# Two cross-attention and expert layers on one core: in the first attention the values are weighed head by head, across group borders

## The chip, the cores and the metric

The kernel runs on one core of a Trainium2 chip. The metric is the device time of one execution in microseconds (us), the median of several. The profile shows one execution; its engines are PE (TensorE, matrix products), DVE (VectorE), ACT (ScalarE), POOL (GpSimd) and SP (which only issues transfers).

## The reference, cut to what matters

Two layers, each a cross-attention and a mixture of experts, on 2048 tokens (2 batches of 1024) of width 256. The change touches the first attention alone:

```python
def _L0_xattn_ref(query, key, value, mask, wq, bq, wk, bk, wv, bv, wo, bo):
    Q = proj(query, wq, bq, sq)          # 16 heads of width 16
    K = proj(key, wk, bk, sk)            # 154 keys
    V = proj(value, wv, bv, sk)
    scores = jnp.einsum('bhqd,bhkd->bhqk', Q, K) / np.sqrt(D_K)
    scores = jnp.where(mask[:, None, :, :] == 0, NEG, scores)
    attn = jax.nn.softmax(scores, axis=-1)
    ctx = jnp.einsum('bhqk,bhkd->bhqd', attn, V)
    return ctx.transpose(0, 2, 1, 3).reshape(b, sq, D_MODEL) @ wo + bo
...
x = x + _L0_xattn_ref(_layernorm(x), ctx_1024, ctx_1024, mask, ...)
x = x + _L0_ffn_ref(_layernorm(x), ...)   # 8 experts, the best 2 of each token
```

## The kernel before, in words

Every engine has its own instruction list, written by hand, and waits on counted semaphores (`pe.wait_ge(S("a0_mx"), n)` waits until n maxima are taken). An engine runs its list strictly in the order written. The order of the calls in the loops over `g` and `u` is therefore the schedule.

The tokens are worked in four groups (`g` 0 to 3, NG) of four tiles (`t`) of 128 tokens. A group of the first attention has these steps.

- Queries. `turn` transposes the normalised tokens, `project_q` makes the queries in two banks of PSUM (there are 8 banks of 512 numbers; which two, `q_bank(g)` says), ACT's `q_parts` and DVE's `q_low` split them in a high and a low half-precision part, and SP's `stack_queries` carries them through memory into `q_stack`. This is done two groups ahead, near the end of group g-2.
- Maxima. `score_max(g, n)` makes scores with the tokens on the partitions, and DVE's `maximum(g, n)` takes the largest of each token and head. This is done one group ahead. Then DVE's `negate`, PE's `turn_max` and ACT's `maxima_turned` bring the maxima into the rows of `edge`.
- Scores. `score(g, u)` makes scores with the keys on the partitions, a unit of 512 tokens at a time: 16 units for the 16 heads' first 128 keys, and 4 units that each hold the last 26 keys of four heads. The units use banks 4 and 5 in turn. ACT takes the exponential of a unit (L1160) into a ring of four, then copies it to half precision (`p_hi`, L1163); DVE forms the rest (`p_lo`, L1690). The exponential of unit u waits for the rest of unit u-4.
- Weighing. `weigh_values(g, t)` multiplies the weights of one tile, all heads, by the values, 40 matrix products for a tile, and ACT's `low_outputs`, DVE's `head_outputs` (L1541, L1542, L1545) add the parts and divide by the sum.
- Output. `turn_out` and `project_out` for each half group (two tiles), and DVE's `update` adds it to `x` (counted by a0_x). The rows then get their statistics (`moments`, `scale_and_shift`), `turn_rows` and `route_rows` make the logits of the experts, DVE's `choose` and `place` (with `route_positions` on PE between them) pick experts and places, and POOL's `split_rows` and `scatter` write the rows to the experts' lists. These run one group late, beside the next group's scores. POOL's `low_parts` makes low parts of the first expert's weights once the scores of group 2 are done.

Before, all 20 units of a group are scored first and kept (`p_hi` and `p_lo` hold 20 units each), and the four `weigh_values` follow at the group's end. The loop of PE:

```python
for u in range(20):
    score(g, u)
    if more and 1 <= u < 13:
        score_max(g + 1, u - 1)
...
weigh_values(g, 0)
weigh_values(g, 1)
if more:
    turn_max(g + 1)
```

The maxima are taken in 12 steps of up to six heads, each over two banks; the steps use banks 0 and 1, and 2 and 3, in turn. The experts' layer begins when the rows of the last group are scattered; that waits for the last `update` of the first attention.

## Time and profile before

| what | value |
|---|---|
| median of 3 executions | 921.59 us (919.04 to 923.31) |
| the profiled execution's own time | 923.3 us |
| its span, first to last instruction | 921.6 us |
| mean granted clock of PE | 0.879 |
| busy over the span | PE 77%, DVE 61%, ACT 44%, POOL 32% |
| first attention, from the first rest of a unit to the last update of x | 58.5 to 264.3 us of the span |

A row of a timeline is: start in us, length in us, engine, line, operation, output and inputs by name with shapes, how many; in brackets the engine's idle time before it and what ended it. The length runs over the pipeline's fill and drain, so that rows on one engine may overlap; the distance of two starts is what one instruction costs in a row of them.

### The profile page before, as it was taken

How to read it: one execution, taken by the hardware profiler on the slowest of the kernel's cores; microseconds unless marked ns; L12 is line 12 of the kernel's file. 1: busy time of each engine (PE TensorE's matmuls, PEld its weight loads, DVE VectorE, ACT ScalarE, POOL GpSimd, SP SyncE). 2: the span in 40 equal slices, each digit the busy share in tenths (PEclk: the TensorE clock that was granted, in tenths of full speed). 3: DMA queues.
4: the chain of work that ended last, by engine and by line, in shares of the span. 5: the costliest groups of instructions: out<-in, count | busy, mean ns of one | idle time of the engine just before them, and what ended most of it. 6: DMA issues, size and time to landing. Idle time of an engine off the chain costs nothing.

```text
span 921.6 us, 19114 instructions
## 1 busy us (share of the span) xinstructions
PE 708.8 (77%) x6266; PEld 552.5 (60%) x6278; DVE 560.0 (61%) x1396; ACT 403.0 (44%) x720; POOL 293.2 (32%) x285
## 2 busy tenths in 40 slices
PE   5676786987744999998997989995762098889882
PEld 4223454554534898887885878895441076767771
DVE  7778586887653645564645646457687445566441
ACT  1135465766430635463545535443443045445331
POOL 6415201416258213122212122121045414333342
PEclk8788898978666999999998999997755589999996
DMA  4661303302336523534535523415023455464332
GB/s 134 122 138 39 58 1 62 135 23 77 118 112 234 149 44 63 145 76 127 126 77 152 143 63 94 107 26 174 23 79 111 160 166 125 103 149 118 54 58 39
DMA packets 68419, 92.25 MB, mean 100 GB/s; under 512 B 14442, under 2 KB 54435, under 8 KB 68348
## 3 DMA queue, kind: packets, MB, share of 16 engines
q1 hardware_dynamic: 41788, 63.37, 23.2%
q0 software_dynamic: 14592, 16.24, 10.4%
q10 hardware_dynamic: 11968, 11.72, 4.9%
q8 instruction: 42, 0.69, 0.3%
q14 instruction: 29, 0.24, 0.1%
HBM read 64.21 MB, written 29.87 MB: 102 GB/s over the span
## 4 chain that ended last, share of the span: by engine, by line
PE 42%; DVE 26%; issue 13%; ACT 8%; DMA 4%; ACTq 2%; POOL 2%; another core or an unknown queue 1%; DVEq 1%; POOLq 0%; SPq 0%
PE ps L659 40%; DVE probs L1690 2%; DVE stats L1357 2%; DVE mx L1553 2%; DVE keys L1768 2%; DVE probs L1773 2%; ACT probs L1163 1%; DMA out_x<-keys,row_to 1%; DMA probs<-rows 1%; POOL rows L612 1%; DVE keys L1747 1%; ACT expo L1160 1%; ACT probs L1241 1%; ACT probs L1245 1%
## 5 line engine op out<-in xcount | busy, mean ns | idle before, releaser
L1768 DVE TENSOR_TENSOR keys<-probs,ps 128x512 f32<-128x512 f32 x122 | 82.7, 686 | 191.6 <-PE ps L659 121.8
L659 PE MATMUL ps<-keys,slot 128*128 128x256 f16 (+1 forms) x1440 | 149.5, 266 | 15.5 <-issue 8.9
L659 PE MATMUL ps<-keys,probs 128*128 128x256 f16 (+1 forms) x1488 | 139.9, 255 | 19.2 <-issue 15.6
L659 PEld LDWEIGHTS ps<-keys,slot 128*128 128x128 f16 x1440 | 128.5, 100 | 35.6 <-issue 17.5
L659 PEld LDWEIGHTS ps<-keys,probs 128*128 128x128 f16 x1488 | 123.6, 98 | 34.6 <-issue 19.9
L575 POOL DMA_INDIRECT attended<-keys,row_to x42 | 68.9, 1641 | 167.6 <-ACT keys L1253 145.4
L1241 ACT ACTIVATE probs<-ps 128x512 f32<-128x512 f32 x122 | 71.4, 598 | 79.9 <-PE ps L659 75.3
L1253 ACT ACTIVATE keys<-ps,carried 128x256 f32<-128x256 f32 x80 | 33.5, 470 | 150.4 <-issue 84.4
L1245 ACT CAST probs<-keys 128x512 f16<-128x512 f32 x122 | 74.8, 614 | 26.8 <-DVE keys L1768 24.2
L1773 DVE TENSOR_TENSOR probs<-keys,probs 128x512 f16<-128x512 f32 x122 | 83.5, 688 | 3.8 <-ACT probs L1245 2.0
L1690 DVE TENSOR_TENSOR probs<-expo,probs 128x512 f16<-128x512 f32 x80 | 61.8, 784 | 33.1 <-ACT probs L1163 29.7
L659 PE MATMUL ps<-slot,probs 128*128 128x256 f16 x636 | 75.6, 273 | 3.4 <-ACT probs L1245 2.3
L659 PE MATMUL ps<-probs 128*128 128x256 f16 x612 | 72.7, 273 | 2.8 <-ACT probs L1245 2.1
L575 POOL DMA_INDIRECT out_x<-keys,row_to x38 | 58.9, 1550 | 48.4 <-ACT keys L1253 41.6
L1160 ACT ACTIVATE expo<-ps 128x512 f32<-128x512 f32 x80 | 48.1, 601 | 52.7 <-PE ps L659 44.1
L659 PEld LDWEIGHTS ps<-slot,probs 128*128 128x128 f16 x636 | 59.7, 98 | 15.2 <-ACT probs L1245 4.6
L659 PEld LDWEIGHTS ps<-probs 128*128 128x128 f16 x612 | 57.5, 98 | 13.9 <-ACT probs L1245 4.6
L571 POOL COPY row_to<-carried 128x2 int32 x40 | 11.9, 298 | 155.3 <-DMA attended<-keys,row_to 55.9
L907 PE MATMUL ps<-identh,probs 128*128 128x128 f16 x336 | 26.5, 224 | 34.2 <-DMA probs<-rows 34.2
L1367 DVE TENSOR_TENSOR probs<-inbox,probs 128x1024 f16<-128x1024 f32 x36 | 43.3, 1222 | 13.4 <-ACT probs L1103 13.4
L659 PE MATMUL ps<-penalties,identb 128*128 128x462 bf16 x96 | 34.5, 360 | 19.2 <-DVE mx L1553 7.7
L1163 ACT CAST probs<-expo 128x512 f16<-128x512 f32 x80 | 49.0, 618 | 0.0
(277 smaller groups left out, 1147.6 us busy)
## 6 DMA issues: line engine op xcount, KB each, us to landing
inbox<-in_W SPq DMA_DIRECT2D x24, 512.0 KB
probs<-rows ACTq DMA_DIRECT2D x44, 260.0 KB
inbox<-in_wg SPq DMA_DIRECT2D x16, 512.0 KB
inbox<-in_wu SPq DMA_DIRECT2D x16, 512.0 KB, 3.8
inbox<-in_wd SPq DMA_DIRECT2D x16, 512.0 KB, 4.2
rows<-zeros SPq DMA_DIRECT2D x16, 260.0 KB
x<-in_x SPq DMA_DIRECT2D x4, 512.0 KB, 6.3
q_out<-queries SPq DMA_DIRECT2D x8, 256.0 KB, 2.1
```

What stands on the lines that cost most here:

```text
L575: pool.indirect_dma_start(out=l.sums, out_offset=bass.IndirectOffsetOnAxis(ap=row_to[:, hf:hf + 1], axis=0), in_=yb[:, hf, :], in_offset=N ...
L659: return pe.matmul(o, l, r, start=start, stop=stop, **kw)
L907: last = pe.transpose(psh[:, 6, part * BLK + hf * P:part * BLK + (hf + 1) * P], x_raw[:, hf, part * P:(part + 1) * P], identh[:, :])
L1160: act.activation(e_ring[:, u % 4, :], ps[:, 4 + u % 2, :], ACT.Exp, scale=float(DK) ** -0.5).then_inc(S("a0_exp"), 1)
L1163: act.copy(p_hi[:, u - 1, :], e_ring[:, (u - 1) % 4, :]).then_inc(S("a0_phi"), 1)
L1241: act.activation(s_act[:, j % 2, :], ps[:, 2 * (j % 2), :], l.act).then_inc(S(r + "_s"), 1)
L1245: act.copy(h_hi[:, 2 * j - 2:2 * j, :].rearrange("p c t -> p (c t)"), h32[:, (j - 1) % 2, :]).then_inc(S(r + "_hh"), 1)
L1253: ins = act.activation(yb[:, hf, :], ps[:, 4 + hf, 0:D], ACT.Identity, scale=carried[:, bass.ds(g, 1), hf, 0:1].rearrange("p b d -> p (b d)"))
L1367: dve.tensor_tensor(w[:, 1, at:at + CH], stage[:, n % STAGES, :], w[:, 0, at:at + CH], ALU.subtract).then_inc(S(f"w_ready{l.n}"), 1)
L1690: dve.tensor_tensor(p_lo[:, u, :], e_ring[:, u % 4, :], p_hi[:, u, :], ALU.subtract).then_inc(S("a0_plo"), 1)
L1768: dve.tensor_tensor(h32[:, j % 2, :], s_act[:, j % 2, :], ps[:, 2 * (j % 2) + 1, :], ALU.mult).then_inc(S(r + "_h32"), 1)
L1773: dve.tensor_tensor(h_lo[:, 2 * j - 2:2 * j, :].rearrange("p c t -> p (c t)"), h32[:, (j - 1) % 2, :], h_hi[:, 2 * j - 2:2 * j, :].rearran ...
```

## The change

The four `weigh_values` at a group's end are gone. The 20 units are reordered as four head groups of five: four heads, then the unit with their last 26 keys. `weigh_unit(k, i)` weighs one unit for all four tiles (8 matrix products) and stands in PE's loop five to seven units behind its score, so that the last head group of a token group is weighed beside the first units of the next. After each head group `low_outputs(k)` and `head_outputs(k)` run for all four tiles, 16 times in all as before and with the same number of elements. The outputs of the weighing keep banks 2 and 3, so that the maxima have only banks 0 and 1: 24 steps of at most three heads, each in one bank, in units 1 to 10 (`max_steps`) instead of 12 steps in units 1 to 12. The rings `p_hi` and `p_lo` hold ten units. `choose` and `place` of group g move from the end of group g+1 into units 2 and 7 of group g+2, `route_rows` to unit 1 of it. In DVE's loop the maxima of unit n+2 now stand ahead of the rest of unit n. Other steps move by some units, and some buffers to other places.

```diff
+QH = 4
+UNITS = 5 * QH
+HELD = 10
+STEPS = 24
...
         def q_bank(g):
-            return 6 if g == 1 else 2
+            return 6 if g else 2
...
+        def weighed_heads():
+            tiles = ps[:, 2:4, :].rearrange("p b (t c) -> p (b t) c", c=D)
+            return tiles[:, :, 0:QH * VW].rearrange("p t (h v) -> p t h v", v=VW)
+
+        def max_steps(u):
+            return range(STEPS * (u - 1) // 10, STEPS * u // 10) if 1 <= u <= 10 else range(0)
+
+        def weighed_at(n):
+            k, step = divmod(n - 7, 5)
+            units = (range(0, 2), range(2, 4), range(4, 5), range(0), range(0))[step] if k >= 0 else range(0)
+            return [(k, i) for i in units if k < QH * NG]
...
+            def weigh_unit(k, i):
+                g, q, n = k // QH, k % QH, 5 * k + i
+                b, slot = g // 2, n % HELD
+                pe.wait_ge(S("a0_plo"), n + 1)
+                if i == 0:
+                    if k:
+                        pe.wait_ge(S("a0_oev"), k)
...
+                for t in range(GT):
+                    o, tk = o4[:, t], slice(t * P, (t + 1) * P)
+                    if i < QH:
+                        mm(o[:, i, :], p_hi[:, slot, tk], v_ext[:, b, QH * q + i, :], i == 0 and t % 2 == 0, False, ...)
+                        last = mm(o[:, i, 0:DK + 1], p_lo[:, slot, tk], v_ext[:, b, QH * q + i, 0:DK + 1], False, False, ...)
...
             for g in range(NG):
-                for u in range(20):
+                for u in range(UNITS):
                     score(g, u)
-                    if more and 1 <= u < 13:
-                        score_max(g + 1, u - 1)
+                    for k, i in weighed_at(UNITS * g + u):
+                        weigh_unit(k, i)
+                    if more:
+                        for n in max_steps(u):
+                            score_max(g + 1, n)
+                    if g >= 2 and u == 1:
+                        route_rows(g - 2, range(GT), g - 1)
...
+                    if ahead and u == 18:
...
+                        project_q("a0", g + 2, w_sb["wq"], q_bank(g + 2))
...
-                weigh_values(g, 0)
-                weigh_values(g, 1)
...
@@ ACT
+                    if u % 5 == 4 and UNITS * g + u >= 9:
+                        low_outputs((UNITS * g + u - 9) // 5)
@@ DVE
+                    if n == 0:
+                        maxima(1)
+                    maxima(n + 2)
+                    dve.wait_ge(S("a0_phi"), n + 1)
+                    dve.tensor_tensor(p_lo[:, n % HELD, :], e_ring[:, n % 4, :], p_hi[:, n % HELD, :], ALU.subtract)...
+                    if u % 5 == 4 and n >= 9:
+                        head_outputs((n - 9) // 5)
+                    if g >= 2 and u == 2:
+                        choose(L[0], g - 2)
+                    if g >= 2 and u == 7:
+                        place(L[0], g - 2)
```

On DVE, at the border of groups 0 and 1, before: the last rests of group 0 (L1690), the queries' low parts (L1531), and the first of the four head outputs; the first rest of group 1 and the first maximum come behind the fourth.

```order
L1690 TENSOR_TENSOR probs<-expo,probs 128x512 x2
L1531 SCALAR_TENSOR_TENSOR queries<-ps,b_bq,queries 128x512 x2
L1690 TENSOR_TENSOR probs<-expo,probs 128x512
L1704 TENSOR_TENSOR gate<-gate,ps 128x32
L1541 TENSOR_TENSOR heads<-ps,heads 128x256
L1542 RECIPROCAL rden<-ps 128x16
L1545 TENSOR_TENSOR heads<-heads,rden 128x256
```

The same place on DVE now, from the last two rests but one of group 0 (L1725 is the rest, L1579 a maximum of one bank, L1559 the queries' low part).

```order
L1725 TENSOR_TENSOR probs<-expo,probs 128x512 x2
L1579 TENSOR_REDUCE mx<-ps 128x3 x2
L1725 TENSOR_TENSOR probs<-expo,probs 128x512
L1569 TENSOR_TENSOR heads<-ps,heads 128x256
L1570 RECIPROCAL rden<-ps 128x16
L1573 TENSOR_TENSOR probs<-heads,rden 128x4x64
L1559 SCALAR_TENSOR_TENSOR queries<-ps,b_bq,queries 128x512 x2
L1579 TENSOR_REDUCE mx<-ps 128x3 x2
L1725 TENSOR_TENSOR probs<-expo,probs 128x512
```

Two maxima of the group after next moved ahead of the group's last rest, one head output stands there in place of four, and the queries' low part comes behind it.

On PE, in unit 11 of group 0, before: the score (slot,keys; turned_masks; edge), and right behind it a maximum step over two banks (penalties; keys,queries), as in each of the units 1 to 12.

```order
L659 MATMUL ps<-slot,keys 128x512
L659 MATMUL ps<-turned_masks,identb 128x512
L659 MATMUL ps<-edge,msel 128x512
L659 MATMUL ps<-penalties,identb 128x462
L659 MATMUL ps<-keys,queries 128x308
L659 MATMUL ps<-keys,queries 128x154
L659 MATMUL ps<-penalties,identb 128x462
L659 MATMUL ps<-keys,queries 128x462
```

On PE, from unit 8 to unit 9 of group 0 now: a maximum step in one bank, then the score of the last keys of four heads, and behind it the weighing of a unit (probs with v_rem; the pair of products comes four times, once for a tile, of which the first stands here).

```order
L678 MATMUL ps<-penalties,identb 128x462
L678 MATMUL ps<-keys,queries 128x462
L678 MATMUL ps<-gate,mean 128x8 x4
L678 MATMUL ps<-slot,k_rest 128x512 x2
L678 MATMUL ps<-edge,mselr 128x512
L678 MATMUL ps<-v_rem,probs 128x132
L678 MATMUL ps<-v_rem,probs 128x4x17
```

The weighing stands between a unit's score and its maximum steps.

On ACT, at the border of groups 1 and 2, before: from the last but one exponential of group 1 to the first two of group 2.

```order
L1160 ACTIVATE expo<-ps 128x512
L1163 CAST probs<-expo 128x512
L1093 ACTIVATE queries<-ps,b_bq 128x512 x2
L1122 COPY xT<-ps 128x1024
L1160 ACTIVATE expo<-ps 128x512
L1163 CAST probs<-expo 128x512 x2
L1110 ACTIVATE xln<-x,nb_r,ry_r 128x256 x4
L1138 COPY heads<-ps 128x256
L1097 ACTIVATE ev<-dv 128x4
L1138 COPY heads<-ps 128x256
L1142 COPY edge<-ps 32x512
L1138 COPY heads<-ps 128x256 x2
```

The same place on ACT now.

```order
L1187 ACTIVATE expo<-ps 128x512
L1193 CAST probs<-expo 128x512
L1164 COPY heads<-ps 128x256
L1151 COPY xT<-ps 128x1024
L1193 CAST probs<-expo 128x512
L1122 ACTIVATE queries<-ps,b_bq 128x512 x2
L1139 ACTIVATE xln<-x,nb_r,ry_r 128x256 x4
L1187 ACTIVATE expo<-ps 128x512 x2
L1193 CAST probs<-expo 128x512
```

Three of four head copies left the border, and the queries' high part (L1122) moved behind the last exponential and the copy of the turned rows (L1151).

## Rows read from the trace of the kernel before

**Rows 1.** Windows: the four groups and the tail (columns in the first line)

```profile
core 0: us, PE busy (x) PEld busy (x) DVE busy (x) ACT busy (x) POOL busy (x), PEclk, DMA share, GB/s
58.50:113.00 54.50, 38.71 (x302) 20.21 (x303) 40.03 (x83) 27.55 (x52) 21.10 (x17) 0.86 0.41 79
113.00:164.30 51.30, 41.48 (x347) 25.41 (x350) 38.23 (x104) 31.31 (x61) 4.56 (x8) 0.93 0.20 48
164.30:208.00 43.70, 38.43 (x332) 24.43 (x333) 36.34 (x101) 30.21 (x57) 14.28 (x18) 0.88 0.17 60
208.00:238.60 30.60, 22.96 (x100) 12.14 (x99) 24.68 (x42) 21.89 (x43) 14.67 (x13) 0.87 0.41 126
238.60:264.30 25.70, 16.57 (x206) 14.20 (x206) 9.85 (x49) 4.51 (x11) 12.16 (x17) 0.62 0.20 66
```

**Rows 2.** Groups of instructions of DVE, 164.3 to 208.0 us, by form

```profile
L1690 DVE TENSOR_TENSOR probs<-expo,probs 128x512 f16<-128x512 f32 x20 | 13.4, 688 | 3.6 <-ACT probs L1163 3.5
L1553 DVE TENSOR_REDUCE mx<-ps 128x6 f32<-128x924 f32 x8 | 8.9, 1114 | 0.0
L1555 DVE TENSOR_REDUCE mx<-ps 128x3 f32<-128x462 f32 x4 | 2.5, 633 | 0.0
L1545 DVE TENSOR_TENSOR heads<-heads,rden 128x256 f32<-128x256 f32 x4 | 1.7, 425 | 0.1
L1541 DVE TENSOR_TENSOR heads<-ps,heads 128x256 f32<-128x256 f32 x4 | 1.7, 424 | 2.9 <-ACT heads L1138 2.8
L1556 DVE TENSOR_REDUCE mx<-ps 128x1 f32<-128x154 f32 x4 | 1.2, 310 | 0.0
L1542 DVE RECIPROCAL rden<-ps 128x16 f32<-128x16 f32 x4 | 1.0, 248 | 0.0
```

**Rows 3.** Timeline of ACT at the border of groups 1 and 2

```profile
145.85 0.60 ACT L1160 ACTIVATE expo<-ps 128x512 f32<-128x512 f32 x1 [3.50 <-PE ps L659]
...
147.84 1.28 ACT L1093 ACTIVATE queries<-ps,b_bq 128x512 f16<-128x512 f32 x2
149.00 1.03 ACT L1122 COPY xT<-ps 128x1024 f32<-128x1024 f32 x1
149.89 0.64 ACT L1160 ACTIVATE expo<-ps 128x512 f32<-128x512 f32 x1
...
162.48 1.24 ACT L1160 ACTIVATE expo<-ps 128x512 f32<-128x512 f32 x2 [0.28 <-PE ps L659]
```

**Rows 4.** Timeline of PE: a projection of queries, and one of logits

```profile
141.49 3.67 PE L659 MATMUL ps<-xT,w_wq 128*128 128x512 f32 x8 [1.55 <-ACT xT L1086]
...
236.34 2.47 PE L659 MATMUL ps<-gate,xT 128*128 128x8 f32 x16 [1.60 <-ACT xT L1122]
```

**Rows 5.** Timeline: a maximum and the step that waits for it

```profile
47.65 1.11 DVE L1553 TENSOR_REDUCE mx<-ps 128x6 f32<-128x924 f32 x1
...
48.82 0.37 PE L659 MATMUL ps<-penalties,identb 128*128 128x462 bf16 x1 [0.33 <-DVE mx L1553]
```

**Rows 6.** Timeline of group 3, while POOL makes low parts

```profile
217.54 8.73 DVE L1690 TENSOR_TENSOR probs<-expo,probs 128x512 f16<-128x512 f32 x3 [0.61 <-issue]
...
218.22 6.29 POOL L561 TENSOR_TENSOR slot<-inbox,slot 128x1024 f16<-128x1024 f32 x3
...
225.16 0.60 ACT L1160 ACTIVATE expo<-ps 128x512 f32<-128x512 f32 x1 [4.58 <-DVE probs L1690]
```

**Rows 7.** Timeline of DVE in the tail: first and last of choose, of place

```profile
242.03 0.18 DVE L1576 COPY lg<-ps 128x32 f32<-128x32 f32 x1
...
244.47 0.17 DVE L1608 TENSOR_TENSOR cumb<-cumb,gsum 128x8 bf16<-128x8 bf16 x1
...
249.73 0.22 DVE L1616 TENSOR_TENSOR ohp<-oh,ps 128x64 f32<-128x64 f32 x1
...
250.85 0.17 DVE L1636 TENSOR_TENSOR xp<-dn,xp 128x4 f32<-128x4 f32 x1
```

**Rows 8.** Timeline of the tail: the last low copy, the last update

```profile
256.26 0.37 ACT L1138 COPY heads<-ps 128x256 f32<-128x256 f32 x1 [7.53 <-remote]
...
263.56 0.69 DVE L1571 TENSOR_TENSOR x<-x,ps 128x512 f32<-128x512 f32 x1 [4.91 <-PE ps L659]
```

More of the change, by code:

```diff
@@ L1172, in _ @@
                         normalise("a0", g + 2, 3)
-                    if g + 2 < NG and u == 15:
+                    if g and u == 12:
+                        out_turned(g - 1, 1)
+                    if ahead and u == 13:
                         x_evac("a0", g + 2, xT)
-                    if g + 2 < NG and u == 18:
+                    if more and u == 16:
+                        maxima_turned(g + 1)
+                    if g and u == 19:
+                        rows_turned(g - 1, range(GT), 0, g)
+                    if ahead and u == 20:
                         q_parts(g + 2)
-                    if g and u == 18:
-                        rows_turned(g - 1, range(GT), 6, g)
                     if g == NG - 2 and u in (4, 7, 9):
@@ L1681, in _ @@
             q_low(0)
-            for n in range(12):
+            for n in range(STEPS):
                 maximum(0, n)
@@ L1706, in _ @@
                                           ALU.subtract).then_inc(S("kv_done"), 1)
[L1707 removed]
+                    if g and u == 12:
                         update(g - 1, 0)
[L1709 removed]
+                    if g and u == 15:
                         update(g - 1, 1)
[L1711 removed]
+                    if g and u == 16:
                         dve.wait_ge(S("a0_x"), 2 * g)
                         moments("r0", (g - 1) * GT, GT)
[L1714 removed]
+                    if g and u == 17:
                         scale_and_shift("r0", (g - 1) * GT, GT)
[L1716 removed]
+                    if ahead and u == 19:
                         q_low(g + 2)
[L1718 to L1727 removed]
+            choose(L[0], NG - 2)
+            head_outputs(QH * NG - 1)
+            place(L[0], NG - 2)
+            update(NG - 1, 0)
             dve.wait_ge(S("a0_x"), 2 * NG - 1)
```

319 lines of the change are left out of this document (145 added, 174 removed).

## The prediction, made before the changed kernel ran

> **What bounds the kernel now.** I read the windows first, cut at the first rest of each group (p_lo, L1690). From there to the last update of x the first attention takes 205.8 us, in pieces of 54.5, 51.3, 43.7, 30.6 and, for the tail behind the last rest, 25.7 [rows 1]. Over these DVE is busy 40.0, 38.2, 36.3, 24.7 and 9.9 us, together 149.1, PE 158 and ACT 115. No engine is full: DVE stands for 56.7 us, 14.5, 13.1 and 7.4 in the first three groups and 21.8 in the last with its tail. The reader is to see that the engines wait for each other, and where.
>
> The first place is the group border. The last exponential of group 1 starts at 149.89, the first of group 2 at 162.48, 12.6 us later, with the weighing between [rows 3]. The second is the tail: behind the last rest at 238.6 come all weighing, choosing and projecting, one after the other, up to 264.25, and the clock there is 0.62, near the half level of 1.2 GHz [rows 1, 8]. The third are PE's long jobs: a projection of queries takes 3.67 us, and the next exponential finds no score for 3.50 us [rows 3, 4].
>
> **The change, part by part.** I sum each group as DVE's work plus DVE's waits, since DVE has the most work in a group that can't be hidden and it ends each unit.
>
> *DVE's work.* A rest costs about 0.61 from start to start, 0.69 alone. A head output is 0.42 + 0.25 + 0.43 less overlap, 1.05. The elements of the 16 head outputs are the same, so is their number. Of the maxima, 8 of 1.11, 4 of 0.63 and 4 of 0.31 a group become 20 of 0.63 and 4 of 0.31 [rows 2]; by the last two rows the overlap of neighbours is some 0.08 each, which leaves 11.2 against 11.6 us, so +0.4 a group. choose is 242.03 to 244.64 and place 249.73 to 251.02 [rows 7], 3.9 together. One head output leaves group 0 and comes to the last. choose and place of group 0 leave group 1, and come to group 2 in the place of those of group 1, which come to group 3. Four maxima (2.1) move ahead of the first rest, from each group to the one before. Work after: group 0 40.0 - 1.05 + 0.4 = 39.4; group 1 38.2 - 3.9 + 0.4 = 34.7; group 2 36.3 + 0.4 - 2.1 = 34.6; group 3 and tail 24.7 + 9.9 + 1.05 + 3.9 = 39.5.
>
> *The start.* The first rest now stands behind four maxima, two of which need the second unit's score and its exponential's bank. They take 2.1 of DVE and about 0.5 of latency: **+2.6**.
>
> *Waits in units 1 to 10.* A step of the maxima starts on PE 0.06 us after the maximum that it waits for ends (47.65 + 1.11, 48.82 [rows 5]); its two products take some 0.57 by my estimate (0.37 to the end of the first, 0.2 for the second), and there are two banks. So a bank comes back 0.63 after it is read, and DVE needs 0.55 for the other: 0.1 a step is lost. Now a score (three products of the same 0.2) and one or two weighings (eight narrow products, put at 0.03 each, 0.24; 160 a group as before) stand between the steps, and a head group's first weighing waits for the reciprocal of the one before, which costs 0.7 to 0.85. I make that 0.9 in group 0, where statistics fill the gaps, 2.8 in group 1, 3.1 in group 2 and 3.5 in group 3.
>
> *Waits in units 11 to 19.* DVE has little there (0.61 a unit and its extras), while ACT needs 1.0 a unit and PE 0.9 with the weighing, and PE's jobs stand in a row: the projection of 3.67 [rows 4], and by estimate two output projections of about 2 and three transposes of about 1. I take 3.9, 7.3 and 5.3 us for the groups 0 to 2. All of this exists before too; the weighing adds to it.
>
> *Waits at the border.* This is new. DVE takes the maxima of unit n+2 ahead of the rest of unit n. At the last unit of groups 0 and 1 these are the first maxima two groups on, whose queries ACT makes behind the group's last copies: exponential, two copies, a low copy, the turned rows 1.03 and the queries 1.28 [rows 3] stand before them, and a step of 0.65 behind. DVE has its own rest 1.7 after the exponential's start, the maxima come at 4.8: 3.1 of waiting in group 1, and 2.2 in group 0, which has no turned rows. In group 2 route_rows waits for the low queries, which DVE makes last; it is 2.47 [rows 4], and with a score, a weighing and a step behind it DVE stands 4.3 more, which I count to group 1. So the border costs 2.2 and 7.5.
>
> *The tail.* Behind the last rest come one head group's weighing (1.3) in place of four tiles', choose, one head output in place of four, and the output path as before. DVE's work there is 8 us (two head outputs, choose, place, two updates, a statistic) and the waits for route_rows, the transposes and two projections 6; the last low copy starts at 256.26 after an idle time of 7.53 that the row puts to no engine here [rows 8]; four tiles' weighing explains some 4.5 of it, and 3 are left, which I keep. Waits in group 3 and tail: 3.5 + 9 = 12.5, against 21.8.
>
> *POOL.* The low parts hold DVE: POOL's three operations run 6.3 us, and one rest takes 7.5 of 8.73 [rows 6]. They now come behind a scatter that starts with place at unit 7 of group 3, some 10 us later, and still within the group; the cost is already in DVE's 24.7 as busy. If this cover were gone, up to 3 us more would show, since ACT has no other unit left to run ahead with.
>
> The Trainium skill (GPSIMD Engine Reference, Specifications) says that POOL's SBUF interface is shared with DVE and contends with DVE operations of two SBUF inputs; a rest is one, a maximum from PSUM is not. By that rule, the trace agrees; it would make the lock free if it fell beside maxima, but group 3 has none.
>
> *Sum.* Start +2.6. Group 0: 39.4 + 7.0 = 46.4, -8.1. Group 1: 34.7 + 17.6 = 52.3, +1.0. Group 2: 34.6 + 8.4 = 43.0, -0.7. Group 3 and tail: 39.5 + 12.5 = 52.0 against 56.3, -4.3. My waits hold none of the short stops in which all engines stand, but those of before do; I add 2.5. Sum -7.0. What follows starts when the rows are scattered and just moves. The profiled execution's own time is 923.3 around a span of 921.6; it gives 916.3. The median of the runs shown is 1.7 lower, 921.6, which gives **914.6**.
>
> **The rivals.**
> *Waits vanish.* The loop of ten units runs without a break over the borders, and the 45.5 us of waits that I keep are estimates of a schedule. If the engines slip past each other and those of groups 0 to 2 halve (33.0 to 16.5), with no stop added, it is 921.6 - 7.0 - 16.5 + 4.5 = 902.6. For it speaks that PE's load is 31 to 38 of 45 to 52 us; against it that PE is in order and carries jobs of 2 to 4 us.
> *Slower: the weighing waits for the reciprocal.* The chain low copy 0.37 [rows 8], sum 0.42, reciprocal 0.25, wait 0.06, two weighings 0.5, step 0.63 is 2.2 us, during which DVE lacks its next maximum. I count 0.8 at the places with maxima and nothing elsewhere. It decides from 0.44 us at each of the 16 head groups; at 0.7, +11: 925.6.
> *Slower: the clock.* Groups run at 0.86 to 0.93 now [rows 1], the tail at 0.62. If the many short waits of two single banks pull three groups to 0.75, PE's 38 to 41 us a group grow by some 15 percent of which two thirds show: 4 each, +12: 926.6. The Trainium skill (TensorE: Matmul & The Clock Gate, A second HAM failure mode) describes such a kernel, with bank after bank and short idles between groups of products. No run here shows it.
> *No change.* The borders only move their wait (before: no unit; after: maxima and logits wait for queries), group 0 gains half of the 8.1, and the rest holds: 918.7.
>
> **How the numbers follow.** Forecast 0.40 (its own range 908 to 920), waits vanish 0.20, reciprocal 0.18, clock 0.07, no change 0.15. A measurement of this kernel can tell about 0.5 percent, 4.6 us, from no change. Faster than 917: 0.34 of the first and 0.20; slower than 926.2: about half of the two slower cases and their far side, with what I did not think of, 0.23; the rest 0.23. The range reaches to the middle of the best case and just past the worst: 902 to 928.
>
> **What would show it.** In the profile after: first rests of the groups at about 61, 107.5, 160 and 203, the last update near 257. PE's gaps in front of weighing products ended by the reciprocal, under 1 us each. A stop of DVE of 2 to 3 us ahead of a maximum at the end of groups 0 and 1, ended by PE, and one of 4 behind the low queries of group 3. Exponentials that follow each other over the border with no more than 6 us. The low parts beside group 3's last units. The prediction is wrong if group 0 isn't shorter by 5 us or more, if a stop longer than 5 us stands at a place not named, or if the tail from the last rest to the last update isn't below 18 us.

## The result and the profile after

The changed kernel takes 942.49 us (median of 4 executions, 940.92 to 945.13) and the kernel before 922.45 on the same chip: ratio 1.0212, interval 1.0177 to 1.0247. It is slower by some 20 us. I had forecast 914.6 and a range of 902 to 928. The profiled execution took 943.6 us for a span of 941.8.

Windows of the changed kernel, cut at the first rest of each group, at the last rest, at the last update of x and at the experts' first product; the first five answer to [rows 1].

```profile
62.00:110.50 48.50, 35.81 (x289) 18.33 (x292) 39.56 (x90) 27.39 (x53) 22.87 (x17) 0.93 0.29 61
110.50:165.60 55.10, 42.09 (x320) 25.54 (x326) 35.74 (x83) 30.42 (x58) 4.48 (x8) 0.91 0.19 36
165.60:213.20 47.60, 33.86 (x301) 20.60 (x306) 35.51 (x106) 29.10 (x54) 12.46 (x14) 0.97 0.30 87
213.20:254.70 41.50, 29.43 (x261) 18.67 (x263) 30.25 (x81) 23.58 (x47) 16.96 (x17) 0.83 0.23 75
254.70:271.50 16.80, 12.83 (x92) 10.51 (x92) 9.25 (x43) 3.48 (x8) 9.93 (x14) 0.59 0.39 123
271.50:309.30 37.80, 15.68 (x70) 15.01 (x71) 17.07 (x79) 8.65 (x19) 28.05 (x30) 0.60 0.56 191
```

DVE's work came out nearly as summed: 39.6, 35.7, 35.5 and, for group 3 with its tail, 39.5, against 39.4, 34.7, 34.6 and 39.5, in all 2.1 us more. The rest of the miss is waiting: inside the attention DVE stood for 59.2 us where I had 45.5. Half of the miss lies behind the attention. The last update of x ends 7.2 us later than before (271.5, 264.3), the first product of the experts 15.6 us later (309.3, 293.75), the end 20.2.

The places of the waits, in four short timelines of the changed kernel. First PE and DVE at the border of groups 1 and 2:

```profile
158.22 3.55 PE L678 MATMUL ps<-gate,xT 128*128 128x8 f32 x16 [4.19 <-DVE queries L1559]
...
153.67 1.18 DVE L1579 TENSOR_REDUCE mx<-ps 128x3 f32<-128x462 f32 x2 [2.80 <-PE ps L678]
...
164.30 1.41 DVE L1579 TENSOR_REDUCE mx<-ps 128x3 f32<-128x462 f32 x2 [6.23 <-PE ps L678]
```

The 2.80 is the stop that I had put at 3.1. The logits wait for the low queries, run at the half clock, and DVE stands 6.23 where I had 4.3. Then group 2, where choose stands between two rests (170.96 and 175.42) and PE waits for the maximum behind it:

```profile
170.96 0.68 DVE L1725 TENSOR_TENSOR probs<-expo,probs 128x512 f16<-128x512 f32 x1
...
174.02 0.17 DVE L1631 TENSOR_TENSOR cumb<-cumb,gsum 128x8 bf16<-128x8 bf16 x1
174.10 1.40 DVE L1579 TENSOR_REDUCE mx<-ps 128x3 f32<-128x462 f32 x3
...
174.79 0.24 PE L678 MATMUL ps<-penalties,identb 128*128 128x154 bf16 x1 [3.12 <-DVE mx L1579]
```

In group 3 a rest beside POOL's low parts takes 6.6 us and not 0.68, and behind it stand a head output, its reciprocal and the weighing; 3 us before, PE had stood for an update of x:

```profile
237.93 7.21 DVE L1725 TENSOR_TENSOR probs<-expo,probs 128x512 f16<-128x512 f32 x2 [3.13 <-issue]
...
237.68 6.30 POOL L580 TENSOR_TENSOR slot<-inbox,slot 128x1024 f16<-128x1024 f32 x3
...
234.94 2.04 PE L678 MATMUL ps<-w_wo,heads 128*128 128x256 f32 x4 [2.61 <-DVE x L1594]
...
245.78 0.58 PE L678 MATMUL ps<-v_ext,probs 128*128 128x33 f16 x16 [5.05 <-DVE rden L1570]
```

Behind the attention ACT stands 3.5 us after PE's last transpose for it has ended by the record (272.16), and its first issue of a transfer of rows to the experts takes 2.88 us:

```profile
275.72 0.58 ACT L1151 COPY xT<-ps 128x512 f32<-128x512 f32 x1 [6.43 <-remote]
...
299.65 2.88 ACTq L1255 DMA_DIRECT2D probs<-rows  x1
...
309.30 1.03 PE L936 MATMUL ps<-identh,probs 128*128 128x128 f16 x8 [12.85 <-DMA probs<-rows]
```

The kernel before issued the same transfer in 0.45 us, at 290.34.

### The profile page after: what moved, and what is told of

It is laid out like the page before. It is cut to its first block, busy times and chain, and to the rows that moved or that the text cites. A ratio compares the mean times of both kernels' runs of the same rounds, so it can differ in the third digit from the quotient of the medians.

```text
span 941.8 us, 19218 instructions
## 1 busy us (share of the span) xinstructions
PE 716.1 (76%) x6257; PEld 556.4 (59%) x6278; DVE 562.2 (60%) x1428; ACT 402.5 (43%) x720; POOL 296.9 (32%) x285
## 4 chain that ended last, share of the span: by engine, by line
PE 46%; DVE 24%; issue 13%; ACT 6%; DMA 3%; ACTq 2%; POOL 2%; another core or an unknown queue 1%; DVEq 1%; POOLq 0%
PE ps L678 44%; DVE mx L1579 3%; DVE probs L1725 2%; DVE stats L1385 2%; DVE keys L1801 2%; DVE probs L1806 1%; DMA probs<-rows 1%; POOL rows L631 1%; DMA out_x<-keys,row_to 1%; ACT probs L1273 1%; DVE keys L1780 1%; ACT probs L1269 1%; ACT probs L1193 1%; DVE slot L1395 1%
## 5 line engine op out<-in xcount | busy, mean ns | idle before, releaser
L678 PE MATMUL ps<-keys,slot 128*128 128x256 f16 (+1 forms) x1440 | 152.2, 269 | 20.2 <-issue 14.4
L1281 ACT ACTIVATE keys<-ps,carried 128x256 f32<-128x256 f32 x80 | 33.6, 470 | 150.5 <-issue 88.6
L1187 ACT ACTIVATE expo<-ps 128x512 f32<-128x512 f32 x80 | 47.6, 599 | 80.0 <-PE ps L678 60.1
L1725 DVE TENSOR_TENSOR probs<-expo,probs 128x512 f16<-128x512 f32 x80 | 62.2, 786 | 29.7 <-ACT probs L1193 21.5
L1579 DVE TENSOR_REDUCE mx<-ps 128x3 f32<-128x462 f32 x96 | 52.0, 580 | 29.7 <-PE ps L678 28.4
L678 PEld LDWEIGHTS ps<-slot,probs 128*128 128x128 f16 x636 | 59.7, 98 | 15.0 <-ACT probs L1273 4.6
L590 POOL COPY row_to<-carried 128x2 int32 x40 | 12.5, 313 | 156.3 <-DMA attended<-keys,row_to 56.8
L936 PE MATMUL ps<-identh,probs 128*128 128x128 f16 x336 | 26.5, 224 | 35.8 <-DMA probs<-rows 35.8
L631 POOL DMA_INDIRECT rows<-xp,slot_s x24 | 25.3, 1053 | 87.4 <-DVE xp L1659 48.6
```

Source lines behind the costliest of these rows:

```text
L631: pool.indirect_dma_start(out=rows, out_offset=bass.IndirectOffsetOnAxis(ap=slot_s[:, g * GT + t, k:k + 1], axis=0), in_=beside_row[g % l. ...
L678: return pe.matmul(o, l, r, start=start, stop=stop, **kw)
L936: last = pe.transpose(psh[:, 6, part * BLK + hf * P:part * BLK + (hf + 1) * P], x_raw[:, hf, part * P:(part + 1) * P], identh[:, :])
L1187: act.activation(e_ring[:, u % 4, :], ps[:, 4 + u % 2, :], ACT.Exp, scale=float(DK) ** -0.5).then_inc(S("a0_exp"), 1)
L1281: ins = act.activation(yb[:, hf, :], ps[:, 4 + hf, 0:D], ACT.Identity, scale=carried[:, bass.ds(g, 1), hf, 0:1].rearrange("p b d -> p (b d)"))
L1579: dve.tensor_reduce(mx[:, t, h0:h0 + k], ps[:, n % 2, 0:k * SK].rearrange("p (h s) -> p h s", s=SK), AX, ALU.max).then_inc(S("a0_mx"), 1)
```

## The experiments

The ratios are to the kernel before, timed together with each kernel on the same chip. From one set of runs to the next its own median lay between 913.8 and 923.6 us, on one and the same chip too, so absolute times of different sets aren't compared. Stretches of a profile are, with that 1 percent in mind. x1 to x4 are one set, x5 to x8 the next (913.8 us before), then x9 to x12 and x13 to x16. "Units 0 to 10" is the time from a group's first rest to its twelfth, "units 11 to 19" from there to the group's last, and "the border" from there to the first rest of the next group.

**Four edits of the changed kernel.** DVE's order undone (x1):

```diff
-                    maxima(n + 2)
                     dve.wait_ge(S("a0_phi"), n + 1)
                     dve.tensor_tensor(p_lo[...], e_ring[...], p_hi[...], ALU.subtract)
+                    maxima(n + 2)
```

> The changed kernel, but on DVE the rest of unit n stands again ahead of the maxima of unit n+2. Theory (waits of the new DVE order): the first rest comes 3.5 us earlier, and the last rest of groups 0 and 1 no longer stands behind maxima that wait for the queries (2.8 us at 153.7 in the changed kernel), so the attention ends 4 to 6 us earlier and the time is 936 to 938.5. Rival (the order is worth having, since a maximum that comes late holds PE, which waits 15 us for maxima in groups 0 to 2): maxima come one rest later, 0.6 us a unit in 30 units of which a third shows, and the time is 943 to 949.

1.0217 (1.0175 to 1.0259), as without the edit. The first rest came 2.3 us earlier (59.7), but the groups 1 and 2 took 106.8 and not 102.8 us, and the last update came 1.9 later. Both theories missed: what it wins at the start it loses later. Whether the rest or the maxima of two units ahead come first on DVE makes no difference to the whole.

POOL's low parts earlier (x2):

```diff
                 split_rows(L[0], g)
+                if g == 1:
+                    pool.wait_ge(S("a0_st"), 20 * (NG - 1))
+                    low_parts(L[0], 0, 0, range(0, STAGES))
                 scatter(L[0], g)
-                if g == 1:
...
```

> The changed kernel, but POOL makes the first expert's low parts ahead of the scatter of group 1 and not behind it, so that they start when the scores of group 2 are done, near 214 us, and not at 237.7. Theory (the 6.3 us of POOL beside a rest cost PE 5.0 us in front of the weighing, because the rest that is held is one that the weighing and a head output stand behind): at the start of group 3 it holds a rest while a choose stands there too, ACT still runs four units ahead, and 1 to 3 us are won: 939.5 to 941.5. Rival (the price is the same wherever a rest falls on it): 942.5, within 1 us. A third: the later scatter of group 1 delays split rows of the groups behind it, and the tail gets 1 to 2 us longer.

1.0255 (1.0224 to 1.0286): nothing gained. The row of 6.7 us at 215.08 now meets a rest and choose, and PE stands 5.7 us for choose's last instruction:

```profile
215.08 6.73 POOL L580 TENSOR_TENSOR slot<-inbox,slot 128x1024 f16<-128x1024 f32 x3
215.60 2.15 DVE L1725 TENSOR_TENSOR probs<-expo,probs 128x512 f16<-128x512 f32 x1 [1.02 <-ACT probs L1193]
...
217.88 0.37 DVE L1613 MAX8 mx<-lg 128x8 f32<-128x8 f32 x4
...
218.85 0.90 DVE L1617 TENSOR_TENSOR dv<-mx 128x4 f32<-128x4 f32 x1
219.78 2.04 DVE L1603 TENSOR_TENSOR dv<-dv,ry_r 128x4 f32<-128x4 f32 x1
...
222.98 0.21 PE L678 MATMUL ps<-selb,earlier 128*128 128x32 bf16 x1 [5.69 <-DVE cumb L1631]
```

The price moved and was not paid less. Two small operations of choose with two inputs in SBUF take 0.90 and 2.04 us here (0.14 and 0.16 in the changed kernel), while MAX8 with one input keeps its 0.37. The rest is held for 2.15 us, one of POOL's three operations, and not for all three as in the changed kernel; why, no run shows.

Logits, choose, gates, positions and place two units later in groups 2 and 3 (x3; `route_rows` in unit 3, `choose` in 4, `place` in 9):

> The changed kernel, but the logits of group g-2 stand on PE in unit 3 of group g and not in unit 1, with choose and the gates two units later, place and the positions too, and the first transposes of the outputs one unit later. Theory (the 4.2 us that PE stands in front of the logits of group 0, and the 6.2 us that DVE stands in front of the maximum behind them, come from the queries' low part, which DVE makes last): both go to under 3 us and the attention is 3 to 4.5 us shorter, 938 to 939.5. Rival (the wait just moves: the steps of units 1 to 3 need banks and DVE anyway): 941.5 to 943.5.

1.0365 (1.0331 to 1.0399), far worse. The border of groups 1 and 2 shrank from 10.9 to 4.6 us as expected; units 0 to 10 of group 2 grew from 27.7 to 35.4, and group 3 up to its last rest from 40.8 to 52.7: POOL's low parts now held the rest ahead of an update of x. DVE and PE there:

```profile
245.01 7.17 DVE L1725 TENSOR_TENSOR probs<-expo,probs 128x512 f16<-128x512 f32 x1 [3.57 <-issue]
252.10 0.68 DVE L1594 TENSOR_TENSOR x<-x,ps 128x512 f32<-128x512 f32 x1
...
252.92 2.04 PE L678 MATMUL ps<-w_wo,heads 128*128 128x256 f32 x4 [10.31 <-DVE x L1594]
```

The lists of PE and ACT shifted (x4):

```diff
+            for _ in range(120):
+                pe.sem_inc(S("pad_pe"), 1)
# and the same 120 on ACT
```

> The changed kernel with 120 instructions on PE and 120 on ACT added at the very start, that only count up a semaphore which nobody waits for, while both engines stand for the first loads. Every later instruction stands 120 places further in its list. From the last update of the attention to the end the changed kernel takes 670.3 us, the kernel before 657.3, with the same code. Theory (the 13 us are stops that depend on where the instructions lie, such as ACT's 3.5 us in front of the turned rows, the transfer issue of 2.9 us, PE's 4.5 us near 585): this piece changes by 3 us or more, in either direction, and the attention by some us too. Rival (the change itself leaves the stretch behind it slower, by clock or by transfers that now meet): it stays within 1.5 us of 670.3.

1.0140 (1.0101 to 1.0180), although the 120 instructions cost 5.6 us at the start (first rest at 67.6). From the last update to the experts it was 32.0 us and not 37.9, and the first issue took 0.44. From the experts' first product on, this profile showed 633.3 us against 632.5. The theory held for the issue, not for ACT's 3.5 us. The profile is of the slowest of four executions (944.3; the others took 933.8 to 938.6), so where most of the median's gain lies isn't seen in it.

**Is it the place in the list?** One edit in both kernels, `act.sem_inc` 60 times in the changed one (x5) and 69 times in the kernel before (x6), where ACT stands idle for the experts' table:

> The changed kernel with 60 instructions added on ACT alone, in the stretch where it stands for the experts' table (they count up a semaphore that nobody waits for, 77 ns each). In four kernels of the new schedule the first issue of a transfer of rows on ACT took 2.5 to 2.9 us and its first packet moved 6.0 us after its start, with a packet of instructions in between; in the kernel before and in the one padded at the start it took 0.45, and the packet moved after 1.1 to 1.4. Theory (a stop that hangs on where this instruction lies in ACT's list): the issue takes 0.45 again, from the last update to the first product of the experts it is 33 us and not 37.9, and the time is 937 to 938.5. Rival (transfers of other queues in flight delay it): still 2.5 us or more, 942.5 within 1.5.

> The kernel before with 69 such instructions on ACT in the same stretch, so that its first issue has the number in ACT's list that it has in the changed kernel (447 in place of 378). Theory (place in the list alone makes the stop): the issue takes 2.5 to 2.9 us, the experts start 4.5 to 5 us later, and the time is 926.5 to 927.5. Rival: the place does not decide it, the issue takes 0.45, and the time is 922 within 1.5.

The changed kernel falls to 1.0122 (1.0082 to 1.0162), the kernel before rises to 1.0079 (1.0055 to 1.0104). The issue with the number 507 in ACT's list, then the one with the number 447 in the kernel before:

```profile
293.53 0.45 ACTq L1257 DMA_DIRECT2D probs<-rows  x1
```

```profile
284.86 2.45 ACTq L1229 DMA_DIRECT2D probs<-rows  x1
```

Packets in the 3.2 us from the issue on, padded changed kernel first, then the padded kernel before (queue, kind, packets, MB, share):

```profile
q1 hardware_dynamic: 268, 0.52, 46.0%
q10 hardware_dynamic: 272, 0.27, 30.9%
```

```profile
q1 hardware_dynamic: 240, 0.52, 63.2%
q14 instruction: 1, 0.01, 1.2%
```

q10 carries the rows. With the number 447 a packet of instructions moves and no packet of rows; with another number the 272 packets are all under way. The stop at the issue comes and goes with the place alone, and both ratios moved by what the theory said or more (0.9 and 0.8 percent). From the last update to the experts the changed kernel now takes 28.2 us, 9.6 less; 6.7 of it are the issue's (2.94 us to the first product against 9.65), the rest is mostly ACT's stop of 3.5 us, which doesn't stand in this profile and can't be the padding's doing, since that comes later. The profile is of one of the two quickest of six executions (918.9; four took 925 to 927), so it shows more than the median gained: from the experts' first product on it took 620.7 us against 632.5, with the same code, in a set in which the kernel before ran 8.6 us faster too.

**The steps alone**, in the kernel before (x7):

```diff
-                    if more and 1 <= u < 13:
-                        score_max(g + 1, u - 1)
+                    if more:
+                        for n in max_steps(u):
+                            score_max(g + 1, n)
...
-                    if more and u < 12:
-                        maximum(g + 1, u)
+                    if more:
+                        for step in max_steps(u + 1):
+                            maximum(g + 1, step)
```

> The kernel before with one part of the change alone: the maxima in 24 steps of one bank, banks 0 and 1, in units 1 to 10; the weighing stays at the group's end. Theory (the steps' price is what the sum counted, 0.4 us a group of DVE and 0.1 us a step of waiting, since DVE works on the bank while PE fills the other): three groups of 2.5 to 3 us and the first 24 steps 2, 7 to 10 us slower, 929 to 932. Rival (steps in a row beside scores are hidden, since units 11 to 19 take up what units 1 to 10 lose): 921 to 925. A second rival (two banks in turn starve DVE at the granted clock, a score and an output projection stand between the steps): 935 or more.

1.0281 (1.0242 to 1.0319), the second rival's size, and by the ratio no less than the whole change. Then with DVE's order of the changed kernel (`max_steps(u + 2)` ahead of the rest; x9):

> The kernel before with the 24 steps of one bank as in the run that made it 2.8 percent slower, but DVE takes the maxima of unit u+2 ahead of the rest of unit u, as in the changed kernel; there they stood one unit ahead and behind the rest. Units 0 to 10 of the groups 0 to 2 took 27.1, 22.9 and 22.1 us before, 33.0, 32.6 and 33.6 with the steps alone, 27.4, 23.0 and 27.7 in the changed kernel. Theory (two banks let PE run ahead of DVE by less than a unit, so each unit becomes one chain of score, exponential, copy, rest and maxima, and the order of DVE is what opens it): they go back to 24 to 28, 23 to 26 and 22 to 26, and the time is 0 to 1 percent over before. Rival (the steps themselves cost, whatever the order, and the weighing of the changed kernel hides it): 30 or more in each group, over 2 percent.

1.0039 (1.0010 to 1.0067), the theory's range. Units 0 to 10 of the groups 0 to 2, steps alone and then with the order:

```profile
59.20:92.20 33.00, 22.18 (x92) 8.56 (x92) 25.77 (x63) 14.06 (x27) 14.16 (x9) 0.89 0.48 94
117.30:149.90 32.60, 23.88 (x117) 12.10 (x118) 20.65 (x37) 14.98 (x29) 0.00 (x0) 0.95 0.00 1
177.30:210.90 33.60, 24.05 (x112) 12.04 (x113) 20.66 (x38) 15.80 (x28) 8.81 (x9) 0.95 0.21 76
```

```profile
63.30:88.80 25.50, 18.01 (x81) 7.55 (x80) 23.55 (x60) 12.74 (x25) 9.42 (x5) 0.87 0.51 104
115.60:139.50 23.90, 20.01 (x107) 10.71 (x106) 18.09 (x35) 13.71 (x27) 0.00 (x0) 1.00 0.00 1
170.30:193.30 23.00, 19.81 (x102) 9.99 (x101) 17.98 (x34) 14.58 (x26) 8.94 (x9) 1.00 0.14 49
```

These stretches flatter the order a little, since with it four of the 24 steps stand ahead of the group's first rest (DVE has 2 to 3 us less in them). From first rest to first rest DVE and PE have nearly the same work in both, 118.3 and 116.3 us of DVE, 124.9 and 119.7 of PE, and the three groups take 172.6 and 152.0 us: the order gives 5 to 10 us a group back. It changes two things, the distance (two units ahead in place of one) and the place beside the rest. The place alone was worth nothing in the changed kernel (x1), so the distance is the likely one; it was not run alone.

**Routing and low parts.** Logits late and low parts early together (x8):

> Both edits of two earlier runs together: the logits two units later, and POOL's low parts ahead of the scatter of group 1. The logits alone made the time 13 us longer, and its trace shows PE standing 10.3 us in front of the second output projection of group 2 for an update of x that stood behind the rest which the low parts held (7.2 us at 245.0). Theory (it was this meeting, not the later logits): with the low parts out of the way group 3 takes 41 us or less and not 52.7, and the time is 938 to 943. Rival (the later place of choose and place itself delays the chain of group 3): 948 or more.

1.0232 (1.0189 to 1.0275) against 1.0365 for the logits alone: group 3 took 44.9 us, 8 less, though not 41. The meeting was most of that loss. Units 0 to 10 of group 2 stayed long, at 35.8 us.

The next three build on the changed kernel with the 60 instructions, x11 on x10 and x12 on x11:

```diff
# x10: group 0's logits (bank 0) and choose in unit 11 of group 2, positions and place in 14
-                    if g >= 2 and u == 1:
+                    if (g, u) in ((2, 11), (3, 1)):
                         route_rows(g - 2, range(GT), g - 1)
# x11: project_out(g - 1, 0) in unit 10, update(g - 1, 0) in 10, the first rest ahead of maxima(1)
# x12: in scatter(L[0], 1), the row of low parts behind it is gone
                 for t in range(GT):
+                    if l.n == 0 and g == 1 and t < STAGES:
+                        low_parts(L[0], 0, 0, range(t, t + 1))
```

> The changed kernel with the 60 idle instructions on ACT (alone 1.2 percent over the kernel before), and the routing of group 0 behind the steps of group 2: logits in unit 11 in bank 0, choose in 11, positions, gates and place in 14; routing of group 1 stays in group 3. Theory (DVE is what limits the units with steps, so choose and place cost their 3.9 us there and a stop of 3.1 us on PE, and the logits at the border 3.6 us and a stop of 4.2): units 0 to 10 of group 2 take 22 to 24 us and not 27.6, the last unit of group 1 under 6 and not 10.9, units 11 to 19 of group 2 some 2 more than 15.7; 8 to 10 us gained, ratio 1.002 to 1.005. Rival (the wait moves to the units behind, where PE has the output projections): ratio 1.010 or more.

> As the run with the routing behind the steps, and two more edits: the very first rest stands ahead of the first maxima of the next group, and the first output projection comes in unit 10 and not 11, its update of x behind the rest of unit 10 and not 12. Theory: the start gets 2 us back, and the stops of PE for the update of x (1.2, 1.6 and 2.6 us in the three groups) go; 3 to 6 us gained over the run it builds on, ratio 0.996 to 1.001. Rival (that PE stands there costs nothing, since ACT has scores enough, and an update among the last steps delays the maxima): no gain but the start's, 2 us.

> As the run before it, and POOL's three low parts of 2.1 us each stand apart, one ahead of each of the first three tiles' scatters of group 1, and not in a row of 6.3 us behind them. Theory (a row of 6.3 us holds one rest of DVE for 6.6 and so the weighing, a head output and PE 5.0 us; one of 2.1 holds it less than ACT and PE run ahead): 3 to 5 us gained, the longest rest under 3 us. Rival (DVE loses the same 6 us in three pieces, and it is what ends the units there): within 1 us of the run before it. If POOL's share of the time is not what holds DVE, no rest is over 0.7 us.

1.0185 (1.0143 to 1.0226), 1.0156 (1.0114 to 1.0198) and 1.0049 (1.0023 to 1.0074). The first missed its theory and landed where the rival had put it. The border shrank to 4.5 us, but units 0 to 10 of group 2 took 29.7 and not 22 to 24, and units 11 to 19 took 21.3 and not some 18, as the rival said. ACT in unit 4 of group 2 in that kernel:

```profile
161.12 0.38 ACT L1170 COPY heads<-ps 128x256 f32<-128x256 f32 x1
167.03 1.04 ACT L1138 CAST slot<-inbox 128x1024 f16<-128x1024 f32 x1 [5.53 <-DMA inbox<-in_wg]
```

The group came earlier, the transfer of the first expert's weights did not. The two kernels with the logits two units later had met it too (3.70 and 2.57 us of ACT at the same copy). The second gained only 0.3 percent: units 11 to 19 of the groups 1 and 2 fell by 2 us each, the start's 1.7 came back as 2.8 in group 0. The third gained 1.1 percent, more than its theory: 6.1 of the 8.5 us between the two profiles lie in group 3 up to its last rest.

**The transfer, the low parts alone, and the reciprocal.** ACT's high parts in units 9, 12 and 14 and not 4, 7 and 9 (x13: as x12, but without x11's edit of the start); the spread low parts alone, in the kernel before (x14) and in the changed one with the 60 instructions (x15); and x13 with the weighing in two units (x16):

```diff
-            k, step = divmod(n - 7, 5)
-            units = (range(0, 2), range(2, 4), range(4, 5), range(0), range(0))[step] ...
+            k, step = divmod(n - 8, 5)
+            units = (range(0, 2), range(2, 5), range(0), range(0), range(0))[step] ...
```

> As the run with the low parts spread, with two differences: the first rest stands behind the first maxima again, as in the changed kernel (that edit had given nothing: the start 1.7 us earlier, the first group 2.7 longer), and ACT makes the high parts of the first expert's weights in units 9, 12 and 14 of group 2, not 4, 7 and 9. In the three kernels with the routing behind the steps ACT stood 4.2 to 5.5 us in unit 4 for the transfer of these weights, which SP issues behind the queries of group 3 whatever the group's start. Theory (the routing moved out of the steps' units is worth its 4 to 5 us, and this transfer took them back): units 0 to 10 of group 2 take 23 to 25 us and not 30, ratio 0.998 to 1.001. Rival (units 0 to 10 are held by DVE's maxima as before, and ACT's wait was beside them): 28 or more, ratio 1.004 or more.

> The kernel before with POOL's three low parts spread over the scatter of group 1, ahead of its first, second and third tile. There a rest was held for 7.5 of 8.73 us, and ACT stood 4.6 us. Theory (the row of three costs in both kernels): units 0 to 10 of group 3 take 15 to 17 us and not 19, 2 to 4 us gained, ratio 0.996 to 0.998. Rival (before, ACT and PE were ahead by four units and had no weighing behind the held rest, so the row was hidden): 1.000 within 0.002.

> The changed kernel with the 60 idle instructions on ACT (1.2 percent over before) and the low parts spread, nothing else. Theory (the row holds the weighing, a head output and the output path of group 3 whatever stands before it): group 3 is 4 to 7 us shorter (units 11 to 19 15 to 17 and not 21.7), ratio 1.005 to 1.008. Rival (the gain of 10 us in the combined run came with the other edits): 1.010 or more.

> As the run with the high parts later, and the weighing of a head group in two units and not three, the first one unit later (two heads, then the other two and the last keys), so that its first product comes a unit after the reciprocal of the head group before. Rival of the prediction (the wait for the reciprocal, which the changed kernel shows 13 times with 0.5 to 1.4 us, 5.0 once, sets the time): 4 to 8 us gained, ratio 0.990 to 0.995. Theory (PE waits there while DVE is what ends the unit): within 2 us of the run it builds on.

- x13: 0.9999 (0.9977 to 1.0021), in the range of the theory; units 0 to 10 of group 2 took 25.7 us (the theory had 23 to 25), 4.3 less than with the high parts early.
- x14: 0.9921 (0.9896 to 0.9946), **faster than both kernels**, and by more than its theory gave. Units 0 to 10 of group 3 took 18.3, not 15 to 17; group 3 with its tail took 47.8 us against 56.3 in the profile of before and 51.4 in the padded one. Up to the last rest that is 27.8 against 29.9 and 28.9 us, 1 to 2 less; the tail alone took 20.0, and without this edit 26.3, 22.5, 21.0 and 24.4 us (before, x6, x7, x9). So the profiles don't show where most of the 0.8 percent lies.
- x15: 1.0091 (1.0055 to 1.0127) against 1.0122. Units 11 to 19 of group 3 fell from 21.7 to 17.1, just short of the theory's 15 to 17. In the whole the gain is within the intervals, so it isn't shown.
- x16: 0.9984 (0.9968 to 1.0000) against 0.9999: PE's stops for the reciprocal went from 11.2 to 1.4 us in the profiles, and the time hardly moved. The rival fell.

POOL's pieces, and the rest beside the first, in x15:

```profile
225.87 2.36 POOL L580 TENSOR_TENSOR slot<-inbox,slot 128x1024 f16<-128x1024 f32 x1 [11.12 <-DVE penalties L1662]
...
231.20 2.15 POOL L580 TENSOR_TENSOR slot<-inbox,slot 128x1024 f16<-128x1024 f32 x1
...
226.53 2.26 DVE L1728 TENSOR_TENSOR probs<-expo,probs 128x512 f16<-128x512 f32 x1 [0.28 <-ACT probs L1194]
```

The longest rest fell from 6.6 to 2.26 us. Beside a row of three operations a rest took 7.53, 6.61 and 7.17 us (before, the changed kernel, x3), in x2 only 2.15; beside a single one it took 1.95 to 3.14 us in x12, x14 and x15. The Trainium skill (GPSIMD Engine Reference, Specifications) says that POOL's interface to SBUF is shared with DVE, with contention for DVE's operations of two SBUF inputs; by that rule, the trace agrees, the choose of x2 included.

## Why the prediction was wrong

By its own sum, in the profiled execution: 916.3 forecast, 943.6 measured, 27.3 apart.

| term | forecast | measured | apart |
|---|---|---|---|
| start | +2.6 | +3.5 | 0.9 |
| group 0 | 46.4 | 48.5 | 2.1 |
| group 1 | 52.3 | 55.1 | 2.8 |
| group 2 | 43.0 | 47.6 | 4.6 |
| group 3 and tail | 52.0 | 58.3 | 6.3 |
| stops of all engines | +2.5 | in the rows above | -2.5 |
| behind the last update | 0 | +13.0 | 13.0 |

DVE's waits apart from its work were forecast at 7.0, 17.6, 8.4 and 12.5 us and came to 8.9, 19.4, 12.1 and 18.8. Group 0 was 6.0 us shorter than before, over the 5 named; it was the only stage that got shorter.

**The step that failed most is "what follows starts when the rows are scattered and just moves".** Of its 13.0 us, 8.4 lie ahead of the experts. The stop at the transfer issue is shown as the cause of 6.2 of them: from the issue to the experts' first product it is 9.65 us (299.65, 309.30) against 3.41 before (290.34, 293.75) and 2.94 in the changed kernel with the number 507 (293.53, 296.47), and giving the kernel before the number 447 cost it 0.79 percent. The change had lengthened ACT's list from 378 to 447 instructions ahead of that issue. This I couldn't read from the trace of before, but I could have allowed for it: a change that adds instructions moves all later ones in their lists. The other 4.7 lie among the experts, where the same code took 625.3 to 632.9 us in the profiles of the changed kernel and of its first three edits, and 620.7 and 621.0 in those of x5 and x8. One profile of each can't tell whether the change costs anything there; this stays open. So does ACT's stop of 3.5 us in front of the turned rows. From the last update's end to ACT's copy it is 0.75 us in the kernel before. In eleven of the thirteen kernels with the new order the profile has 2.0 to 4.0 us more, and no more in x5 and x8; in the five with the old order it has at most 0.6 more. The padding of x4 left it in place, and that of x5 comes behind it. Not all of it shows: the issue starts 28.2 us after the last update and 26.1 in the kernel before, 2.1 later, which with the 6.2 is the 8.4.

**Group 3 and tail, 6.3.** The sum has a term for waits in units 11 to 19 of the groups 0 to 2 and none for group 3: up to its last rest it allowed DVE 3.5 us of waiting, and DVE waited 11.3. The step behind it was "the cost is already in DVE's 24.7 as busy". It counted POOL's hold on a rest as DVE's time alone. In the new order the weighing of a head group waits for a reciprocal that stands behind that rest, so that PE stood 5.05 us, more than the "up to 3 us more" allowed. That wait is seen in the profile; what it cost in the whole is not shown: spreading the three operations gave 0.8 percent in the kernel before and 1.1 in the combined one, but in the changed kernel alone 0.3, which is not clear of noise. The tail itself was right: 16.8 us, under the 18 named.

**Group 2, 4.6.** I had moved choose's and place's 3.9 us into this group as work and gave them no wait. But PE had run ahead only as far as two banks let it: it stood 3.12 us behind choose. Units 0 to 10 took 27.7 us against 22.1 before. That choose is the cause is argued from this. Moving the routing behind the steps alone made nothing better (1.0185 against 1.0122). Together with the high parts late enough for their transfer, the first output projection a unit earlier and the low parts spread, it took the changed kernel from 1.0122 to 0.9999; the parts of this weren't all run alone.

**Group 1, 2.8.** The mechanism was right, both stops were named; 1.0 of it is work, and the second stop was 6.23 and not 4.3. The logits ran at a granted clock of 0.50, the half level, after PE had stood 2.40 and then 4.19 us, and took 3.55 us against the 2.47 of [rows 4]. The exponentials on both sides of the border came 5.8 us apart (149.04 and 154.84), as named, but the stop stood behind them: ACT then waited 6.67 us for the next score.

**Steps.** "0.1 a step is lost" was near the truth only with DVE's order: in the kernel before, units 0 to 10 took 25.5, 23.9 and 23.0 us with it, 33.0, 32.6 and 33.6 without, and 27.1, 22.9 and 22.1 with the old steps. I had the order right in the sum but never priced it, and the change hung on it.

**The rivals.** The reciprocal's wait was there, seven times with 0.78 to 1.43 us and once with the 5.05 of group 3. That is more than the 0.44 at which it was to decide, but at half of the places, and a unit more of slack, tried on x13, was worth 0.15 percent, not clear of noise. The clock wasn't it: the groups ran at 0.93, 0.91, 0.97 and 0.83 against 0.86, 0.93, 0.88 and 0.87 before, on the whole no lower. The second failure mode that the Trainium skill describes (TensorE: Matmul & The Clock Gate, A second HAM failure mode) isn't shown here.

**Slips in the sum.** The rival of vanishing waits adds 4.5 us that no term explains; with no stop added, as it says, it comes to 895.6 and not 902.6. The maxima's overlap at 0.08 each gives some 0.6 us a group more, not 0.4. Neither bears on the miss.

## What to carry to other kernels

When a step moves on a full engine, count who waits behind it, not only its length: 2.6 us of choose between maxima kept PE waiting for 3.1, and a 6.3 us row of POOL holds whatever stands behind the rest beside it. Try such rows in pieces: this was the one edit that made the kernel before faster. Ask of every group that comes earlier which transfer it now overtakes. And a change that adds instructions shifts everything behind it: before a difference of 1 percent is put down to the schedule, shift one list by some idle instructions and time it again.

## What the runs showed of the hardware

- A transfer issue on ACT took 2.45 to 2.90 us where it has the number 447 in the list, in six kernels of both schedules, and 0.44 to 0.45 where the number is 378, 507 or 567, in twelve. In the four packet counts taken over the first 3.2 us (before, changed, x5, x6), either rows or a packet of instructions moved, never both. From these counts I argue that the list's own instructions hold the issue up; which numbers are hit beyond these four, no run shows.
- A DVE operation with two inputs in SBUF that runs beside POOL's is held: a rest of 0.68 us took up to 7.53. An operation of one input (MAX8, 0.37 us) was not.
- PE's semaphore can rise long after its products end by the record: in the changed kernel the last transpose ends at 272.16, its semaphore rises at 275.70 and ACT starts at 275.72. I found no cause.
- Executions of one kernel on one chip spread by 4 to 14 us; one profile of each can't tell where.
